# Second attention of a four-layer kernel: scores kept on chip per 128-token tile instead of per head group

## What is computed

```python
qkv = (x @ W_qkv).reshape(B, S, 3, H, Dh)
q, k, v = (q[:, :, m], k[:, :, m], v[:, :, m])
qs = q.reshape(B, H, nseg, seg, Dh)
ks = k.reshape(B, H, nseg, seg, Dh)[:, :, :, ::dil]     # 64 keys of 128
scores = jnp.einsum('bhnqd,bhnkd->bhnqk', qs, ks) * scale
out = jnp.einsum('bhnqk,bhnkd->bhnqd', softmax(scores), vs)
x = layernorm(x + out @ W_out)
```

## Time and profile before

| | us |
|---|---|
| time, median of 3 runs (lowest, highest) | 814.04 (807.41, 815.55) |
| the profiled execution's own time | 815.33 |
| its span | 813.5 |
| mean granted TensorE clock over the span | 0.907 |
| PE, DVE, ACT, POOL busy, share of the span | 84%, 79%, 54%, 19% |

### The profile page before, as it was taken

The page is one execution under the profiler, slowest core; times in us unless marked ns, Lnnn a source line. Parts: engine busy times, 40 slices in busy tenths (PEclk is TensorE's granted clock), DMA queues, the critical chain, the costliest instruction groups (busy, mean ns, idle before and its releaser), DMA issues.

```text
span 813.5 us, 16682 instructions
## 1 busy us (share of the span) xinstructions
PE 684.7 (84%) x5898; PEld 442.2 (54%) x5898; DVE 638.8 (79%) x1134; ACT 441.3 (54%) x961; POOL 157.0 (19%) x291
## 2 busy tenths in 40 slices
PE   7578888888888888897556689489999998998883
PEld 4223333333333333345435568479999997997652
DVE  2789999999999999945445436789999995554996
ACT  3059999999999999964422235401211114454442
POOL 6401000000000000003321005701111112122563
PEclk9569999999999999999855558579999999999998
DMA  6711111111111110000366820000000000000000
GB/s 194 219 23 32 32 31 32 31 32 31 32 31 32 31 32 2 3 2 10 87 195 147 186 58 2 0 1 0 1 1 0 0 0 1 0 0 1 15 14 26
DMA packets 25737, 31.87 MB, mean 39 GB/s; under 512 B 5144, under 2 KB 20888, under 8 KB 24376
## 3 DMA queue, kind: packets, MB, share of 16 engines
q1 hardware_dynamic: 24328, 29.42, 14.5%
q0 software_dynamic: 1344, 1.58, 0.7%
HBM read 23.25 MB, written 7.34 MB: 38 GB/s over the span
## 4 chain that ended last, share of the span: by engine, by line
PE 50%; ACT 19%; issue 11%; DVE 10%; DMA 6%; POOL 2%; SPq 2%; DVEq 0%; POOLq 0%; ACTq 0%
ACT probs L1252 16%; PE ps_hi L792 12%; PE ps_lo L1084 7%; PE ps_lo L1086 6%; PE ps_lo L1085 6%; DMA q_rep<-mrow 4%; PE ps_hi L806 3%; DVE probs L1863 2%; PE ps_hi L1144 2%; PE ps_hi L1135 1%; DVE mx L1550 1%; ACT mrow L1207 1%; PE ps_lo L1126 1%; DVE st L1559 1%; PE ps_hi L836 1%
## 5 line engine op out<-in xcount | busy, mean ns | idle before, releaser
L1550 DVE TENSOR_REDUCE mx<-ps_lo 128x2 f32<-128x1024 f32 x256 | 306.3, 1224 | 8.7 <-PE ps_lo L769 5.6
L1252 ACT ACTIVATE probs<-ps_hi 128x512 f32<-128x512 f32 x512 | 278.0, 596 | 41.7 <-PE ps_hi L792 29.3
L806 PE MATMUL ps_hi<-probs,v_blk 128*32 128x256 f32 x2048 | 164.7, 393 | 5.7 <-ACT mrow L1207 5.5
L792 PE MATMUL ps_hi<-q,k 28*128 28x512 f32 x512 | 129.5, 500 | 30.0 <-ACT probs L1252 14.7
L769 PE MATMUL ps_lo<-k,q 26*128 26x512 f32 x512 | 133.3, 515 | 6.3 <-DVE mx L1550 4.2
L1797 DVE SCALAR_TENSOR_TENSOR tok_cur<-ps_lo,w_cur,tok_cur 128x384 f32<-128x384 f32 x240 | 127.8, 608 | 6.1 <-PE ps_lo L1086 4.7
L1084 PE MATMUL ps_lo<-w_hi,op_hi 128*128 128x384 f32 (+1 forms) x304 | 108.1, 356 | 19.9 <-DVEq L1758 10.1
L792 PEld LDWEIGHTS ps_hi<-q,k 28*128 28x128 f32 x512 | 48.7, 183 | 139.9 <-ACT probs L1252 115.9
L1085 PE MATMUL ps_lo<-w_lo,op_hi 128*128 128x384 f32 (+1 forms) x304 | 105.5, 347 | 0.0
L1086 PE MATMUL ps_lo<-w_hi,op_lo 128*128 128x384 f32 (+1 forms) x304 | 105.4, 347 | 0.0
L806 PEld LDWEIGHTS ps_hi<-probs,v_blk 128*32 128x32 f32 x2048 | 42.0, 108 | 70.9 <-ACT probs L1252 59.2
(11 more groups left out here) (251 smaller groups left out, 859.5 us busy)
## 6 DMA issues: line engine op xcount, KB each, us to landing
q<-q_parts SPq DMA_DIRECT2D x30, 192.0 KB
q_rep<-q_parts SPq DMA_DIRECT2D x8, 576.0 KB
k<-k_parts SPq DMA_DIRECT2D x32, 96.0 KB
k_rep<-k_parts SPq DMA_DIRECT2D x24, 96.0 KB
q_parts<-qk_hi SPq DMA_DIRECT2D x8, 256.0 KB, 5.3
q_parts<-qk_p SPq DMA_DIRECT2D x12, 128.0 KB, 3.4
...
```

What stands on the lines that cost most here:

```text
L792: mm = pe.matmul(bank(4 + (2 * n + a) % 3), k0[rows, k_at:k_at + P], q0[rows, h * QN:(h + 1) * QN], start=True, stop=True)
L806: mm = pe.matmul(o_bank()[32 * r:32 * r + 32, 0:OW], v_all[:, at:at + 32], probs0[:, n % P_RING, r * OW:(r + 1) * OW], start=(kb == 0), st ...
L1252: act.activation(probs0[:, n % P_RING, a * QN:(a + 1) * QN], bank(4 + (2 * n + a) % 3), ACT.Exp).then_inc(s0_free, 1)
L1550: dve.reduce_max(mx2[:, j % 2, :, i, kh], bank(2 * (m % 2), 2).rearrange("p (a n) -> p a n", a=2), AX_X).then_inc(max0_done, 1)
```

## The change

The second attention now goes tile by tile, 16 tiles t, without bf16 parts, scratch memory or transfers. The stages of a tile:

- POOL `head_keys(t)`: from the 64 keys of a tile (all 128 channels on partitions) it makes 512 columns, eight copies of the keys, each multiplied by a 0/1 mask that keeps one head's 8 channels in either half of 64 partitions.
- PE `seg_scores(t)`: two fp32 matmuls over 64 rows each (partitions 0 to 63, and 64 to 127), 512 columns each: all 16 heads' scores, tokens on partitions, in two banks.
- DVE `seg_less_max(t)`: maximum per head, then a second pass subtracts it and writes SBUF. ACT `seg_exp_of(t)`: exponential of 1024 numbers.
- PE `seg_T(t, half)`: four fp32 transposes each; ACT `seg_T_copy` copies each half back to SBUF; PE `seg_out(t)`: eight fp32 matmuls with the transposed probabilities as weights and 32 columns of values moving. DVE `seg_o(t)` divides; the tokens are on partitions already, so `heads_tile` goes.

Tiles 0 to 6 use banks 0 to 3; from 7 on odd tiles use 4 to 7. Tiles 0 to 2 lie among the norms of the stage ahead; 3 to 15 run in a loop behind `qkv_products(3)`. `project` waits for all 16 tiles; `w_hi` is copied one piece per tile from tile 8 on; the expert weights' transfers are issued in one go. The mask (`strip`) is made once, at the start, from row sums of the identity.

```diff
...
+HALF = 64
+NK = QN // 2
+M_RING = 2
...
+        p_seg = probs[:, 0, 0:2 * S].rearrange("p (u n) -> p u n", u=2)
+        pT_seg = probs[:, 0, 2 * S:4 * S].rearrange("p (u n) -> p u n", u=2)
+        qk = probs[:, 1, 0:NQ * (QN + NK)].rearrange("p (q n) -> p q n", q=NQ)
+        k_heads = probs[:, 1, NQ * (QN + NK):].rearrange("p (u n) -> p u n", u=M_RING)
...
+        def seg_bank(t, n, count=1):
+
+            return bank((4 if t >= 6 and t % 2 else 0) + n, count)
+
+        def before(t):
+
+            return t - 1 if t <= 6 else t - 2
 
...
-            for q in range(2):
-                store_q1(q)
-            sp.wait_ge(const_set, 9)
-            sp.wait_ge(s0_ps, NU)
-            stored1(0)
-            for s in range(2):
-                load_rep(s)
-            for s in range(2, RING):
-                load_rep(s)
-            for q in range(2, NQ):
-                store_q1(q)
-            load_mrow(0)
-            load_mrow(1)
             sp.wait_ge(ot0_ps, 2 * NQ)
-            for i in range(RING):
+            for i in range(PIECES):
...
+            def head_keys(t):
+
+                q, at = t // QUAD, QN + t % QUAD * KSEG
+                if t == 0:
+                    pool.wait_ge(strip_set, 1)
+                pool.wait_ge(qk_set, q + 1)
+                if t >= M_RING:
+                    pool.wait_ge(seg_ps, t - M_RING + 1)
+                pool.tensor_tensor(k_heads[:, t % M_RING, :].rearrange("p (h k) -> p h k", h=8),
+                                   qk[:, q, at:at + KSEG].unsqueeze(1).broadcast_to([P, 8, KSEG]),
+                                   strip[:].unsqueeze(2).broadcast_to([P, 8, KSEG]), ALU.mult).then_inc(k_heads_set, 1)
+
...
-            fill(k_rep1[64:96, :].bitcast(words), two_ones)
-            root(1, 1)
-            store_k1(0)
-            root(0, 2)
-            pool.wait_ge(ln_std[0], 3)
             pool.wait_ge(p0_free, NU)
             blocks(0, NS * KB)
-            store_k1(1)
+            head_keys(0)
+            root(1, 1)
+            head_keys(1)
+            root(0, 2)
             root(0, 3)
             root(1, 2)
+            head_keys(2)
             root(1, 3)
-            store_k1(2)
-            store_k1(3)
-
-            pool.wait_ge(sim_root, 1)
-            pool.tensor_tensor(sim_n[:], sim_n[:], phalf[:, 0:E], ALU.pow).then_inc(sim_root_done, 1)
+            for t in range(3, NT):
+                head_keys(t)
+                if t == 5:
+                    pool.wait_ge(sim_root, 1)
+                    pool.tensor_tensor(sim_n[:], sim_n[:], phalf[:, 0:E], ALU.pow).then_inc(sim_root_done, 1)
+
...
+            def seg_scores(t):
+
+                q, at = t // QUAD, t % QUAD * P
+                pe.wait_ge(k_heads_set, t + 1)
+                pe.wait_ge(v_sb[1], q + 1)
+                if t == 7:
+                    pe.wait_ge(sim_root, 1)
+                if t:
+                    pe.wait_ge(seg_less, before(t) + 1)
+                for half in range(2):
+                    rows = slice(HALF * half, HALF * half + HALF)
+                    mm = pe.matmul(seg_bank(t, half), qk[rows, q, at:at + P], k_heads[rows, t % M_RING, :],
+                                   start=True, stop=True)
+                mm.then_inc(seg_ps, 1)
+
+            def seg_T(t, half):
+
+                pe.wait_ge(seg_exp, t + 1)
+                pe.wait_ge(qk_set, NQ if t >= 7 else 2)
+                pe.wait_ge(v_sb[1], NQ if t >= 7 else 2)
+                if half or t:
+                    pe.wait_ge(seg_pT_sb, 2 * t + 1 if half else 2 * before(t) + 2)
+                for n in range(QUAD):
+                    at = (QUAD * half + n) * P
+                    mm = pe.transpose(seg_bank(t, 2)[:, n * P:(n + 1) * P], p_seg[:, t % 2, at:at + P], ident_sb[:])
+                mm.then_inc(seg_pT_ps, 1)
+
+            def seg_out(t):
+
+                pe.wait_ge(seg_pT_sb, 2 * t + 2)
+                if t:
+                    pe.wait_ge(ot_read, before(t) + 1)
+                for pair in range(8):
+                    mm = pe.matmul(seg_bank(t, 3)[:, pair * 32:(pair + 1) * 32], pT_seg[:, t % 2, pair * P:(pair + 1) * P],
+                                   vblk(t, pair), start=True, stop=True)
+                mm.then_inc(seg_out_ps, 1)
+
+            def vblk(g, pair):
+                at = ((g + KB) % NT * 8 + pair) * 32
+                return v_blk[:, at:at + 32]
+
...
             wo_products(2)
+            seg_scores(0)
             heads_T(1, 1, 0, 8)
...
             ffn_products(2)
+            seg_T(0, 0)
+            seg_scores(1)
+            seg_T(0, 1)
             ffn_T(3)
             x2_T(2)
+            seg_out(0)
             ffn_products(3)
+            seg_T(1, 0)
+            seg_scores(2)
+            seg_T(1, 1)
             qkv_products(2)
+            seg_out(1)
             x2_T(3)
+            seg_T(2, 0)
+            seg_scores(3)
+            seg_T(2, 1)
+            seg_out(2)
             qkv_products(3)
...
+            pe.wait_ge(sim_sq, 1)
+            pe.wait_ge(qk_set, 3)
+            pe.matmul(flip_bank(2)[:, 0:E], ones[:], rt[0][:, 0, :], start=True, stop=True).then_inc(sim_ss, 1)
+            for t in range(3, NT):
+                ahead = t + 1 if t < 6 else t + 2
+                seg_T(t, 0)
+                if ahead < NT:
+                    seg_scores(ahead)
+                seg_T(t, 1)
+                seg_out(t)
+                if t == 5:
+                    seg_scores(7)
 
...
-                    pe.wait_ge(ot_read, min(NT, max(4 * q + 4, 9 + q)))
+                    pe.wait_ge(ot_read, NT)
...
+            def seg_exp_of(t):
+
+                act.wait_ge(seg_less, t + 1)
+                act.activation(p_seg[:, t % 2, :], p_seg[:, t % 2, :], ACT.Exp).then_inc(seg_exp, 1)
+
+            def seg_T_copy(t, half):
+
+                act.wait_ge(seg_pT_ps, 2 * t + half + 1)
+                if t >= 2:
+                    act.wait_ge(seg_out_ps, t - 1)
+                copy(pT_seg[:, t % 2, half * QN:(half + 1) * QN], seg_bank(t, 2)).then_inc(seg_pT_sb, 1)
 
...
+            for t in range(3, NT):
+                seg_exp_of(t)
+                for half in range(2):
+                    seg_T_copy(t, half)
+                if t == KB:
+                    act.wait_ge(ld_we, PIECES * 16)
+                if t >= KB:
+                    n = t - KB
+                    copy(w_hi[:, n * WC:(n + 1) * WC], big[:, n * WC:(n + 1) * WC]).then_inc(w_hi_set, 1)
...
+            def seg_less_max(t):
+
+                scores = seg_bank(t, 0, 2).rearrange("p (h k) -> p h k", h=H)
+                dve.wait_ge(seg_ps, t + 1)
+                dve.reduce_max(mx[:, t % 2, :], scores, AX_X).then_inc(seg_max_done, 1)
+                dve.wait_ge(seg_max_done, t + 1)
+                if t >= 2:
+                    dve.wait_ge(seg_pT_ps, 2 * (t - 1))
+                dve.tensor_tensor(p_seg[:, t % 2, :].rearrange("p (h k) -> p h k", h=H), scores,
+                                  mx[:, t % 2, :].unsqueeze(2).broadcast_to([P, H, KSEG]), ALU.subtract).then_inc(
+                    seg_less, 1)
+
+            def seg_o(t):
+
+                o = seg_bank(t, 3)[:, 0:8 * 32].rearrange("p (r two c) -> p r two c", two=2, c=16)
+                r = rec[:, t % 2, :].rearrange("p (r two) -> p r two", two=2)
+                dve.wait_ge(seg_out_ps, t + 1)
+                link(dve.reciprocal(r, o[:, :, :, DH]))
+                dve.tensor_tensor(xT[:, t * D:(t + 1) * D].rearrange("p (r two d) -> p r two d", two=2, d=DH),
+                                  o[:, :, :, 0:DH], r.unsqueeze(3).broadcast_to([P, 8, 2, DH]), ALU.mult).then_inc(
+                    ot_read, 1)
 
...
+            for t in range(4, NT):
+                seg_less_max(t)
+                seg_o(t - 1)
...
```

## The result

The forecast was 849 with a range of 806 to 876 and a chance of 0.74 for slower. The profiled execution is the fastest of the four, 842.53, with a span of 840.7 us; before, the profiled execution took 815.33 and had a span of 813.5. So the two profiles differ by 27.2 us and the medians by 31.7.

What follows compares the result with a forecast made beforehand. PE was taken as the bound at both clocks. Loop start 436 + loop 96.4 + division 0.55 + transposes 3.68 = 536.6 against 501.25, 35.4 us later, hence 849 on the scale of medians; range 806 to 876.

Steps and rivals of the forecast that it cites:

- the mean clock: PE's clock in the loop of tiles 3 to 15: the old stage's 0.56 carries over, giving 96.4 us.
- the start of the loop: Tile 3 after the norms: 10 us of added work hidden, 14 of 24.1 push the last `qkv_products` back, start at 436.

Runs made afterwards that it cites:

- experiments 2: Changed kernel with each loop tile's output product moved behind the next tile's transposes: 826.15 us, ratio 1.0183.
- 3: Changed kernel with transposed probabilities and values in bf16, so an output has 8 records instead of 16, rounded more coarsely: 819.72 us, ratio 1.0075.
- 8: Kernel before the change, with the maxima's load issued ahead of the wait for scores and the large repeated load on its queue: 810.69 us, ratio 1.0003.
- 10: Changed kernel with outputs behind the next tile's transposes, a 256-column filler product per loop tile, and fillers at the loop's entry: 822.31 us, ratio 1.0128.
- 11: Kernel of 10 with the last two tiles made dense by outputs between transpose halves and further fillers: 825.79 us, ratio 1.0136.

## What to carry to other kernels

Price a replacement by PE at both clocks, and take as its clock neither the old stage's nor a pure one unless the mixture of work is the same: here the mean clock was the term that moved the sum. Check each term against its own row, too: the start of the loop came out right from two wrong ones. Where PE is busy for 88% and its clock is still low, try a useless product or some transposes in the gap before removing work, and try more than one kind: here 13 products of 256 columns made the kernel 11 to 14 us faster, and thinner ones nothing. Before counting on the end of a wait, ask which transfer or pass is waited for next; in experiments 2, 3, 8, 10 and 11 one stood right behind. And compare stretches, not absolute times: code that was the same up to a point reached it 14.6 us apart.
